# All low parts of the probabilities on GpSimd, and VectorE on PSUM

## The reference

```python
q = _rope(q); k = _rope(k)                       # 64 wide
qk = jnp.einsum('bghsd,bgxpd->bghsp', q, k) * DQK ** (-0.5)
qk = jnp.where(causal, qk, -jnp.inf)
attn = jax.nn.softmax(qk, axis=-1)
o = jnp.einsum('bghsp,bgxpd->bghsd', attn, v)
```

## Time and profile before

| | |
|---|---|
| median of 3 launches | 2225.39 us (2225.27 to 2226.03) |
| profiled execution | 2226.72 us, span of instructions 2224.9 us |
| PE, DVE, ACT, POOL busy | 91%, 70%, 45%, 61% of the span |
| mean granted clock of TensorE | 0.982 |
| attention | from about 100 to 1665 us; a group lasts 190 to 200 us |

### The profile page before, as it was taken

One profiled execution on the slowest core, in us unless ns is written; L12 is line 12 of the kernel. 1 busy time (PEld: TensorE's weight loads), 2 busy tenths in 40 slices (PEclk: granted clock), 3 DMA queues, 4 the chain that ended last, 5 costly groups with the idle time before them and its releaser, 6 DMA issues. The chain is left out here.

```text
span 2224.9 us, 61534 instructions
## 1 busy us (share of the span) xinstructions
PE 2015.6 (91%) x22015; PEld 1226.3 (55%) x22015; DVE 1549.4 (70%) x2914; ACT 998.9 (45%) x2281; POOL 1348.4 (61%) x1470
## 2 busy tenths in 40 slices
PE   2589999988999999899999889999987988999998
PEld 1356665665666566566656656665663443444443
DVE  8479878967986896798689679868963774222221
ACT  3245655554565555456555545655552111211210
POOL 5467777776777777677777767777770442311311
PEclk9999999999999999999999999999998999999999
DMA  5432233223223322322332232233216540000000
GB/s 174 139 51 46 40 68 69 44 43 70 47 43 68 59 44 52 73 48 40 68 59 43 53 71 47 43 68 61 43 38 224 199 162 36 1 19 19 0 19 19
DMA packets 307602, 139.78 MB, mean 63 GB/s; under 512 B 253664, under 2 KB 291296, under 8 KB 305760
## 3 DMA queue, kind: packets, MB, share of 16 engines
q1 hardware_dynamic: 307296, 135.79, 26.8%
HBM read 50.53 MB, written 25.17 MB: 34 GB/s over the span
## 5 line engine op out<-in xcount | busy, mean ns | idle before, releaser
L833 POOL TENSOR_TENSOR pl<-p 128x512 f16<-128x512 f32 (+3 forms) x801 | 759.3, 961 | 182.0 <-ACT p L667 179.1
L762 DVE TENSOR_REDUCE mpart<-a_ps 128x1 f32<-128x512 f32 (+3 forms) x1288 | 717.2, 596 | 154.2 <-PE a_ps L581 84.5
L667 ACT ACTIVATE p<-a_ps 128x512 f32<-128x512 f32 (+3 forms) x1283 | 660.1, 531 | 333.2 <-PE a_ps L596 183.7
L612 PE MATMUL a_ps<-v,p 128*128 128x65 f16 x4352 | 531.4, 193 | 38.7 <-POOL pl L833 22.1
L614 PE MATMUL a_ps<-v,p 128*128 128x64 f16 x4352 | 532.1, 195 | 0.0
L616 PE MATMUL a_ps<-v,pl 128*128 128x65 f16 x4352 | 528.6, 193 | 0.0
L612 PEld LDWEIGHTS a_ps<-v,p 128*128 128x128 bf16 x4352 | 410.4, 97 | 163.8 <-DVE pl L754 33.6
L578 PE MATMUL a_ps<-k_hl,q_hh 128*128 128x512 f16 (+3 forms) x1288 | 445.7, 350 | 54.6 <-issue 23.2
L754 DVE TENSOR_TENSOR pl<-p 128x512 f16<-128x512 f32 (+2 forms) x482 | 449.2, 935 | 30.1 <-ACT p L667 30.1
L595 PE MATMUL a_ps<-q_hh,k_hl 128*128 128x512 f16 (+3 forms) x1283 | 447.7, 349 | 18.4 <-DMA q_lm<-qk_lo 18.4
L614 PEld LDWEIGHTS a_ps<-v,p 128*128 128x128 bf16 x4352 | 407.6, 98 | 81.7 <-issue 0.7
(11 more groups left out here) (98 smaller groups left out, 2708.0 us busy)
## 6 DMA issues: line engine op xcount, KB each, us to landing
attn_scratch<-o_turn SPq DMA_DIRECT2D x64, 256.0 KB, 3.0
p_att<-attn_scratch SPq DMA_DIRECT2D x32, 512.0 KB, 4.4
raw<-ffn_t SPq DMA_DIRECT2D x12, 1024.0 KB, 4.9
wraw<-w_in_t SPq DMA_DIRECT2D x9, 768.0 KB, 6.0
resid_scratch<-xin SPq DMA_DIRECT2D x4, 1024.0 KB, 4.3
raw<-w_out_t SPq DMA_DIRECT2D x1, 4096.0 KB, 15.0
x<-resid_scratch SPq DMA_DIRECT2D x4, 1024.0 KB, 8.0
out<-x SPq DMA_DIRECT2D x16, 256.0 KB, 2.0
```

The source lines that it names most:

```text
L612: nc.tensor.matmul(o, weights, v[:, par, j, 0:VU], start=(j == 0 and t == 0), stop=False, skip_group_check=True)
L667: nc.scalar.activation(p32[:, i % RING, r * P:CHUNK], sbank(i)[:, r * P:CHUNK], ACT.Exp, scale=SCALE).then_inc(exp_done, 1)
L762: nc.vector.reduce_max(mpart[:, u % 2, t, kk:kk + 1], side_bank(part, ("piece", ahead, u, i))[:, 0:width], AX.X)\
L833: nc.gpsimd.tensor_tensor(pl[:, i % RING, cols], p32[:, i % RING, cols], p_high[:, i % RING, cols], ALU.subtract).then_inc(low_pool, 1)
```

## The change

- POOL makes the low parts of all 160 steps (`low_part`), DVE none. One semaphore `low_ready` replaces two.
- The scaled result `onorm` is gone. ACT scales and rounds to the high part in one operation for each of the four query tiles (64 columns each), and DVE makes the low part from `osb`, the reciprocal and the high part in four operations of 64 columns, queued at `LOW_OUT_LAG` + 2 steps after the unit's end.
- PE no longer adds the causal mask to the diagonal pieces (L581). DVE adds it: the reduction of a diagonal piece becomes one operation that adds `causal` (16-bit, in SBUF) to the piece in PSUM, writes the sum into `masked`, and gives the maximum. A memset of one column stands ahead of each, and a wait on the piece two before.

```diff
-                    last = nc.tensor.matmul(bank[:, 0:width], ..., start=True, stop=(kk < c))
-                    if kk == c:
-                        last = nc.tensor.matmul(bank[:, width - P:width], big, mask_qk, start=False, stop=True)
-                    last.then_inc(maxs_ready, 1)
+                    nc.tensor.matmul(bank[:, 0:width], ..., start=True, stop=True)\
+                        .then_inc(maxs_ready, 1)
...
                 def unit_high(u):
-                    act.wait_ge(o_scaled, g * UNITS + u + 2)
+                    act.wait_ge(o_rden, g * UNITS + u + 2)
                     wait_turned(act, g, u)
-                    nc.scalar.activation(unit_part(0, u), onorm[:, u % 2], ACT.Copy).then_inc(o_high, 1)
+                    for t in range(TPC):
+                        last = nc.scalar.activation(unit_part(0, u)[:, t], osb[:, u % 2, t, 0:DH], ACT.Copy,
+                                                    scale=rden[:, u % 2, t:t + 1])
+                    last.then_inc(o_high, 1)
...
+                    if kk < c:
+                        nc.vector.reduce_max(mpart[:, u % 2, t, kk:kk + 1], bank, AX.X).then_inc(maxs_used, 1)
+                    else:
+                        if ahead or n >= 2:
+                            dve.wait_ge(maxs_used, gg * PIECES + n - 1)
+                        nc.vector.memset(credit[:, 13 + n % 2:14 + n % 2], 0.0)
+                        nc.vector.tensor_tensor_reduce(masked[:, n % 2, 0:width], bank, causal[:, CHUNK - width:CHUNK], 1.0, -LEAST,
+                                                       ALU.add, ALU.max, mpart[:, u % 2, t, kk:kk + 1]).then_inc(maxs_used, 1)
...
+                def unit_low(u):
+                    dve.wait_ge(o_high, g * UNITS + u + 2)
+                    wait_turned(dve, g, u)
+                    for t in range(TPC):
+                        last = nc.vector.scalar_tensor_tensor(unit_part(1, u)[:, t], osb[:, u % 2, t, 0:DH], rden[:, u % 2, t:t + 1],
+                                                              unit_part(0, u)[:, t], ALU.mult, ALU.subtract)
+                    last.then_inc(o_norm, 1)
...
-                    if slot(part, n - LOW_LAG)[0] in DVE_STEPS[DVE_HEAD:]:
-                        low_part(slot(part, n - LOW_LAG)[0])
...
+                    if step is not None and step - LOW_OUT_LAG in FIRST_STEP:
+                        unit_low(FIRST_STEP.index(step - LOW_OUT_LAG) - 1)
...
                 for n in range(len(part) + 2):
                     step = slot(part, n - 1)[0]
-                    if step is not None:
-                        if step in POOL_STEPS[POOL_HEAD:]:
-                            low_part(step)
-                        if step - OUT_LAG in FIRST_STEP[1:]:
-                            unit_scale(FIRST_STEP.index(step - OUT_LAG) - 1)
-                        if step - LOW_OUT_LAG in FIRST_STEP:
-                            unit_low(FIRST_STEP.index(step - LOW_OUT_LAG) - 1)
+                    if step is not None and step >= HEAD:
+                        low_part(step)
```

More of the change, by code:

```diff
@@ L44 @@
 VW = VL + DH
+LEAST = 3e37
 def normalise(nc, x, rms_w, resid_dram, yh, yl, ident, ahead):
@@ L231 @@
 SUM_LAG = 2
-LOW_LAG = 3
 HI_LAG = 5
@@ L236 @@
 HEAD = 3
-POOL_STEPS = [i for i in range(STEPS) if i % 8 in (1, 3, 4, 6, 7)]
-DVE_STEPS = [i for i in range(STEPS) if i not in POOL_STEPS]
-DVE_HEAD, POOL_HEAD = (sum(i < HEAD for i in steps) for steps in (DVE_STEPS, POOL_STEPS))
 def step_of(i):
@@ L392, in attention @@
         rden = sb("rden", [P, 2, TPC], F32)
-        onorm = sb("onorm", [P, 2, TPC, DH], F32)
         o_hl = sb("o_hl", [P, 2, 2, TPC, HG, DH], F16)
@@ L396, in attention @@
         credit = sb("credit", [P, 16], F32)
+        causal = sb("causal", [P, CHUNK], BF16)
+        masked = sb("masked", [P, 2, CHUNK], BF16)
         ps = ctx.enter_context(nc.psum_tensor("a_ps", [P, 8, 512], F32))
@@ L404, in attention @@
         ones_set = sem("ones_set")
+        causal_set = sem("causal_set")
         rows_set = sem("rows_set")
@@ L423, in attention @@
         exp_done = sem("exp_done")
-        low_dve = sem("low_dve")
-        low_pool = sem("low_pool")
+        low_ready = sem("low_ready")
         pv_done = sem("pv_done")
@@ L428, in attention @@
         o_rden = sem("o_rden")
-        o_scaled = sem("o_scaled")
         o_high = sem("o_high")
@@ L577, in max_piece @@
                     width = CHUNK if kk < c else (t + 1) * P
-                    last = nc.tensor.matmul(bank[:, 0:width], q_hh[:, c % 2, h, t * P:(t + 1) * P],
-                                            k_hl[:, par ^ ahead, kk * CHUNK:kk * CHUNK + width], start=True, stop=(kk < c))
-                    if kk == c:
-                        last = nc.tensor.matmul(bank[:, width - P:width], big, mask_qk, start=False, stop=True)
-                    last.then_inc(maxs_ready, 1)
+                    nc.tensor.matmul(bank[:, 0:width], q_hh[:, c % 2, h, t * P:(t + 1) * P],
+                                     k_hl[:, par ^ ahead, kk * CHUNK:kk * CHUNK + width], start=True, stop=True)\
+                        .then_inc(maxs_ready, 1)
                 def scores(i, ahead=0):
@@ L607, in values @@
                     pe.wait_ge(exp_done, g * STEPS + i + 1 + EXP_AHEAD)
-                    wait_low(pe, g, i)
+                    pe.wait_ge(low_ready, g * STEPS + i + 1)
                     for t in range(first_query_tile(c, j), TPC):
@@ L737, in _ @@
             nc.vector.memset(v[:, :, :, DH:DH + 1], 1.0).then_inc(ones_set, 1)
+            nc.vector.memset(causal[:, 0:CHUNK - P], 0.0)
+            nc.vector.tensor_scalar(causal[:, CHUNK - P:CHUNK], mask_qk, LEAST / 3e4, None, ALU.mult).then_inc(causal_set, 1)
+            dve.wait_ge(causal_set, 1)
+            nc.vector.memset(osb[:, 1], 0.0)
+            nc.vector.memset(rden[:, 1], 0.0).then_inc(o_rden, 1)
             for n, (s, ahead) in enumerate(((qk_low, TILES_KEPT), (exp_done, EXP_AHEAD),
@@ L761, in reduce_piece @@
                     dve.wait_ge(maxs_ready, gg * PIECES + n + 1)
-                    nc.vector.reduce_max(mpart[:, u % 2, t, kk:kk + 1], side_bank(part, ("piece", ahead, u, i))[:, 0:width], AX.X)\
-                        .then_inc(maxs_used, 1)
+                    bank = side_bank(part, ("piece", ahead, u, i))[:, 0:width]
+                    if kk < c:
[6 more added lines that the diff above has]
+                                                       ALU.add, ALU.max, mpart[:, u % 2, t, kk:kk + 1]).then_inc(maxs_used, 1)
                     if i < KEY_TILES[u] - 1:
@@ L794, in group @@
                         weights_low(0, kt)
-                for n in range(len(part) + LOW_LAG):
+                for n in range(len(part) + 2):
                     for piece in slot(part, n - 1)[2]:
@@ L808, in group @@
                         unit_reciprocal(FIRST_STEP.index(step - OUT_LAG) - 1)
-                for i in DVE_STEPS[:DVE_HEAD]:
-                    low_part(i, ahead=int(part is SLOTS))
+                    if step is not None and step - LOW_OUT_LAG in FIRST_STEP:
+                        unit_low(FIRST_STEP.index(step - LOW_OUT_LAG) - 1)
                 if part is SLOTS:
                     unit_reciprocal(UNITS - 1)
+                if part is LAST:
+                    unit_low(-1)
             group(0, 0, OPENING)
@@ L817, in _ @@
                     group(pair * 2 + par, par, SLOTS)
+            group(GROUPS, 0, LAST)
         @block.gpsimd
         def _(pool):
-            nc.gpsimd.memset(onorm[:, 1], 0.0).then_inc(o_scaled, 1)
             nc.gpsimd.memset(qk_lo[:, :, 0:HG, :, 1, :], 0.0).then_inc(rows_set, 1)
@@ L833, in low_part @@
                     nc.gpsimd.tensor_tensor(pl[:, i % RING, cols], p32[:, i % RING, cols], p_high[:, i % RING, cols],
-                                            ALU.subtract).then_inc(low_pool, 1)
+                                            ALU.subtract).then_inc(low_ready, 1)
                 def rope_sum(ahead, t):
@@ L875, in group @@
                         qk_low_part(*job[1:])
-                for i in POOL_STEPS[:POOL_HEAD if part is not LAST else 0]:
+                for i in range(HEAD):
                     low_part(i, ahead=int(part is SLOTS))
-                if part is SLOTS:
-                    unit_scale(UNITS - 1)
-                if part is LAST:
-                    unit_low(-1)
             group(0, 0, OPENING)
@@ L886, in _ @@
                     group(pair * 2 + par, par, SLOTS)
-            group(GROUPS, 0, LAST)
 def output_projection(nc, raw, ffn_t, ident, attn_dram, resid_dram, tern, scale, x2, xh, xl):
```

22 lines of the change are left out of this document (removed).

## The result

The median of four launches is 2367.63 us (2358.75 to 2369.88); the kernel before, on the same chip, has 2225.71 us. The ratio is 1.0629, with the interval 1.0602 to 1.0657: 6.3% slower, 142 us. The forecast was 2248 us with a range of 2188 to 2292, so the sign was right and the size was a sixth: 23 us forecast, 142 measured. The profiled execution took 2358.75 us, with a span of 2356.9 us and a mean granted clock of 0.957 (0.982 before).

A forecast was written before the change was run, and what follows sets the result against it. PE and DVE were taken as full in units 8 to 11, PE as nearly full in units 12 to 15. Terms of +2.6 us a group, times eight +21, plus +2 for the key chain, on 2225.4 gave 2248 us (2188 to 2292).

The forecast's parts named there:

- The sum per group: Adds the forecast gains and losses of one attention group: total +2.6 us, times eight +21 us.
- Units 2 to 5: Term for this stretch: DVE 4.1 us over, partly absorbed by four side banks and neighbours' slack: +2.4 us (0 to 4.1).
- four banks at 1.0 to 1.1 us a step: Units 6 to 11: banks give PE 4.2 us against 4.4 of DVE block and reduction, about +0.3 us each.
- The turns: DVE's four 64-column operations per unit wait behind POOL's low parts: 3.7 us a unit in units 8 to 11, 2.9 in 2 to 5.
- the rival in which the operations slip through: DVE's four small operations per unit pass through POOL's gaps (0.85 us a unit), relieving DVE: 2189 us, chance 0.32.
- Whole instruction by whole instruction: POOL and DVE operations reading two SBUF tiles alternate, one full instruction each: 1.6 us a pair in the normalising stage.
- Units 6 to 11: Term for six units where DVE's block and next reduction slightly outlast PE's banks: +2.0 us a group (0 to 4).
- Units 12 to 15: Term for the group's end: POOL becomes the bound, 69.6 us in place of 68.48: +1.2 us a group (0 to 3).
- The masks: DVE pays 0.16 us per diagonal piece; PE loses mask products, worth -1.3 us a group where it bounds (0 to -3.4).
- Low-part waits of DVE: PE's waits on low parts made by DVE, 13.8 us in all, go away: -1.7 us a group.
- GpSimd waiting for DVE's rope products: Much slower rival: in units 12 to 15 POOL waits for rope products queued behind DVE's unit operations: 2288 us, chance 0.12.
- The factor of two for GpSimd: Rival: a full-width low part costs GpSimd about 1.3 us, felt in units 8 to 15: 2416 us, chance 0.01.

The follow-up runs named there:

- Experiment 4: Changed kernel, with DVE's four 64-column operations per unit placed one in each of four successive steps instead of in a row: 2306.11 us, 1.037.
- experiment 12: Changed kernel, with POOL waiting once per unit until DVE's four operations on the unit's result are through: 2266.32 us, 1.0188.
- experiments 2: Changed kernel, with the causal mask of the maxima's pieces added by TensorE again and DVE only reducing: 2348.74 us, 1.0561.
- 3: Changed kernel, with ScalarE also writing the scaled result and DVE making a unit's low part in one 256-column operation, not four: 2286.76 us, 1.0283.
- experiment 14: Changed kernel, with TensorE's mask products kept as well, so the mask is added twice: 2362.1 us, 1.0623.
- experiment 8: Changed kernel, with eight DVE operations of 32 columns per unit's low part instead of four of 64: 2610.63 us (one launch).
- experiment 5: Kernel before, with all low parts of the probabilities on POOL; unit's result stays on GpSimd and ScalarE, mask on TensorE: 2274.48 us, 1.0228.
- experiment 9: Kernel before, with GpSimd making all low parts in units 0 to 7 and five of eight after them: 2218.52 us, 0.996.
- experiment 11: Kernel before, with masked maxima on DVE and TensorE's mask products kept, so the mask is added twice: 2235.66 us, 1.0045.
- experiment 7: Kernel before, with only the unit's result split between ScalarE and DVE; low parts and mask stay where they were: 2305.86 us, 1.0373.
- experiment 6: Kernel before, with masked maxima on DVE as the only part of the change (result scaled in place in osb): 2251.7 us, 1.0132.

## Why the prediction was right in sign and wrong in size

**The step that failed** is "The sum per group", in its first term: "Units 2 to 5: DVE 4.1 us over; four side banks and the slack of its neighbours absorb a part: +2.4 (bounds 0 and 4.1)". It measured +9.2 us as a mean of six groups (+8.1 in the sixth), and units 0 and 1, which have no term in the sum, +3.8. That is +13.0 us a group where the sum has 2.4; by eight it is 85 us of the 120 that are missing. The failed reasoning is the bound: it took DVE's excess of *busy time* as the most that the stretch could grow. DVE's busy time came out below the forecast, and the stretch is 5.6 us longer than it. What costs is the length of one block against the few banks in front of it. The prediction gave four banks 4.2 us ("four banks at 1.0 to 1.1 us a step"). In the sixth group TensorE ran on for 1.05 us after the block of unit 2 had begun, for 1.5 in unit 5, for 1.7 and 2.6 after the two that stopped it in unit 10: in units 2 and 3 it makes two pieces a step, and elsewhere the banks are partly used up when the block begins. So a block of 2.4 us stopped TensorE for 2.0, and one of 3.65 for 2.4. And the time isn't made up: TensorE is idle for 10.1 us of the stretch (3.4 before), and DVE, which it waits for, for 5.6 us itself. Experiment 4 (same operations apart: -62 us) and experiment 12 (same place, shorter block: -101 us) show both halves of it.

The +3.8 of units 0 and 1 go with the long hold at the end of the group before. They take 13.3 to 16.4 us in the five kernels where an operation is held for over 10 us in unit 15 (after, experiments 2, 3, 4 and 14), and 10.5 to 12.5 in all others, experiment 8 with its longer blocks and no hold among them (means of groups 2 to 7; 11.5 before).

**The turns** were half right. The mean of 979 ns and the 3.7 us a unit lie in the forecast (3.1 us a unit in units 2 to 5 of the sixth group for 2.9, and 3.3 in units 8 to 11 for 3.7; there five results fall, where the prediction counted four), and the rival in which the operations slip through (2189 us) is excluded. "Whole instruction by whole instruction" is not what they do: there are holds of 10.75 us, one a group, in unit 15. Two-input operations that the change leaves alone are hit as well (weight low parts, 7.0 us in experiment 5). The earlier trace rows show alternation where both engines have a row of equals; the prediction carried that over to a POOL with a backlog of low parts.

**Units 6 to 11**: forecast +2.0, measured +0.4, a sum of -3.0 in units 6 and 7, where DVE's relief is real (experiment 9 has all of it), and +3.4 in units 8 to 11, where four blocks of +0.33 should have cost 1.3. Unit 10 alone goes from 16.3 to 20.9 us: in the sixth group TensorE waits 2.3 and 1.7 us there behind two ordinary blocks of 3.3 and 3.6 us.

**Units 12 to 15**: forecast +1.2 (0 to 3), measured +2.7. POOL is busy for 68.39 of 71.20 us (69.6 forecast). Within bounds; the stretch is not quite POOL alone.

**The masks**: DVE's price was right, 483 ns mean for 520 operations plus 80 and 59. The sign of the term (-1.3) was wrong: alone it costs 28.8 us, taken out of the change it gives 19 back. Why is not shown beyond what experiment 11 shows.

**Low-part waits of DVE** (-1.7): the waits of the earlier trace rows for DVE's low parts are gone, as predicted, and 120 us of waits for its maxima stand in their place.

**What each part costs** alone: low parts 51.6, mask 28.8, split 82.9 us, together 163 where the whole change costs 142. They overlap: alone, the split makes DVE the bound of units 8 to 11 (60.63 us busy), which it is not once the low parts are gone (55.29).

**The other rivals.** GpSimd waiting for DVE's rope products (2288 us) is not seen: those waits are 32.1 us, 26.6 before. The factor of two for GpSimd is excluded, a full-width low part being 1053 ns on average.

**What stays open.** The clock's share: the mean went from 0.982 to 0.957, experiment 11 shows a case in which it goes with the larger part of a loss, and experiment 14 did not bring it back. It has a bound: from the first exponential to the last the clock stands at its lower level for 37.5 us before and for 116.0 after, and at half speed the difference is worth 39 us at most (an estimate). In experiment 7 it is 27.3 us, less than before, and that kernel is 82.9 us slower; in experiment 12 it is 54.6 us, so of the 101 us that the wait gives back at most 31 can be the clock. So most of the loss is not the clock; whether its part prolongs the waits or follows from them is open. What decides when POOL keeps the port is open as well. The profiled executions are 132.0 us apart, of which 128 are in the mean over groups 2 to 7 times eight and 3.8 come before the first exponential; the other 10 of the 142 us are that the profiled execution after (2358.75 us) is the fastest of its four.

## What to carry to other kernels

An operation's duration and an engine's busy share say too little about one that stands in a queue: compare the length of the whole block with the time that the buffers ahead of it hold, in the stretch where they are used up fastest, and count the stop in full from there. Keep two-input SBUF operations of VectorE few, wide and away from an unbroken row of GpSimd work, or let GpSimd pause for them; their price goes by the instruction and not by the columns. Moving work to GpSimd pays where it has gaps on both sides (one line, units 0 to 7: 0.996), and stops paying before it is full.

## What the hardware showed that was not expected

- Of GpSimd and VectorE one can be passed over for long. A 64-column operation waited 10.75 us for twelve instructions of GpSimd end to end, a weight operation 7.1 us, a 256-column one 10.4; in the same kernels others get in after one. The holds come at the same step of every group, GpSimd's pause ended the one shown above, and experiment 8 has none. What decides between the two cases was not found.
- Halving the width of such an operation brings the mean of 979 down to 718 ns and the median of 887 to 830, not to half.
- The maximum with an added mask from PSUM takes what a plain reduction takes (682 against 678 ns for 512 columns), and 80 ns more for reading the accumulator.
- Four copies of 64 columns with a scale from SBUF take ScalarE 343 ns each, 1.4 us a unit, where 0.85 was assumed; DVE waited for them for 1.1 us in the whole span.
- Less work for TensorE made a kernel slower: without 520 mask products experiment 6 is 16 us slower than experiment 11 (20 by each one's own kernel before), with a granted clock of 0.85 in place of 1.00 at the head of a group. The same edit in the kernel after did next to nothing (experiment 14).
